# Expert stage of an adaLN mixture-of-experts layer: each 128-row half of a tile gets its own pair of experts, and the layer-one bias is read by a computed address

## The reference

```python
h = layernorm(x) * (1 + ca) + sa
x = x + ga * attn(h)               # gated linear scan, 32 x 256 tokens of 128 channels
h = layernorm(x) * (1 + cb) + sb
logits = h @ gate_w.T + gate_b      # E = 8 experts
probs = softmax(logits); topk = top_k(probs, 2)
h1 = relu(h @ w1[e] + b1[e])        # 128 -> 512, for each of the two chosen experts e
y  = h1 @ w2[e] + b2[e]             # 512 -> 128
x = x + gb * (p_a * y_a + p_b * y_b)
```

## Time and profile before

| | |
|---|---|
| median of 3 runs | 510.71 us (509.54 to 510.82) |
| the profiled execution (span from first to last instruction) | 521.0 us |
| PE busy | 418.3 us (80%) |
| DVE busy | 442.3 us (85%) |
| ACT busy | 300.5 us (58%) |
| POOL busy | 218.9 us (42%) |
| granted TensorE clock, mean | 0.896 |
| first transpose of the expert stage | 211.5 us |
| tiles run in the expert stage | 46 (92 output writes of 128 rows), 30 straight and 8 loop turns of 2 |

### The profile page before, as it was taken

How to read it: one execution, slowest core, us unless ns; L and a number is a source line. 1 busy time by engine, 2 the same in 40 slices (tenths; PEclk the granted TensorE clock), 3 DMA queues, 4 the chain that set the end, 5 groups by cost and what they waited for, 6 DMA issues and landing times.

```text
span 521.0 us, 14959 instructions
## 1 busy us (share of the span) xinstructions
PE 418.3 (80%) x4292; PEld 344.1 (66%) x4293; DVE 442.3 (85%) x1275; ACT 300.5 (58%) x757; POOL 218.9 (42%) x325
## 2 busy tenths in 40 slices
PE   2868897968865730699999999999999899999960
PEld 2435564545534630499989889998888888888860
DVE  5989999768668773999999999999999899899960
ACT  1538987677753600366667666666666555555530
POOL 7053334757776566013443333443334333333331
PEclk9969999889776555699999999999999999999985
DMA  7535443523312233313333222333223222222210
GB/s 230 160 108 163 120 151 132 184 92 124 123 63 109 111 129 141 90 46 82 88 101 104 84 76 80 80 93 86 75 76 78 76 73 67 71 73 73 67 39 0
DMA packets 48138, 51.04 MB, mean 98 GB/s; under 512 B 5454, under 2 KB 41759, under 8 KB 48082
## 3 DMA queue, kind: packets, MB, share of 16 engines
q1 hardware_dynamic: 39968, 33.17, 22.9%
q0 software_dynamic: 7040, 16.93, 9.0%
q10 hardware_dynamic: 1074, 0.23, 0.2%
HBM read 27.43 MB, written 24.70 MB: 100 GB/s over the span
## 4 chain that ended last, share of the span: by engine, by line
PE 38%; DVE 20%; issue 19%; POOL 14%; DMA 2%; another core or an unknown queue 1%; SPq 1%; ACT 1%; DVEq 0%; POOLq 0%; ACTq 0%
POOL sorted_rows L562 10%; PE bank L1468 6%; PE bank L1465 6%; PE bank L1466 6%; PE bank L1449 6%; PE bank L1451 5%; PE bank L1450 5%; DVE xs L1230 4%; PE bank L1461 2%; DVE xn L905 2%; PE bank L1435 2%; DVE hT L1243 2%; DVE st L845 2%; DVE a L1248 1%
## 5 line engine op out<-in xcount | busy, mean ns | idle before, releaser
L586 POOL DMA_INDIRECT out_dram<-tg,midx x92 | 105.9, 1151 | 199.8 <-DVE tg L1251 185.8
L748 ACT ACTIVATE xs<-bank,bcols 128x256 f32<-128x256 f32 x368 | 139.4, 492 | 22.7 <-PE bank L1451 22.3
L1465 PE MATMUL bank<-w2hi,xs 128*128 x736 | 122.7, 220 | 0.0
L1466 PE MATMUL bank<-w2hi,w2f 128*128 x736 | 122.6, 220 | 0.0
L1232 DVE TENSOR_TENSOR w2f<-xs 128x1024 f16<-128x1024 f32 x92 | 112.7, 1225 | 3.2
L1468 PE MATMUL bank<-w2lo,xs 128*128 x736 | 101.7, 220 | 0.0
L1449 PE MATMUL bank<-xh,w1hi 128*128 128x256 f16 x368 | 101.4, 276 | 0.3 <-ACT xs L748 0.3
L1450 PE MATMUL bank<-xl,w1hi 128*128 128x256 f16 x368 | 101.2, 275 | 0.0
L1451 PE MATMUL bank<-xh,w1lo 128*128 128x256 f16 x368 | 101.2, 275 | 0.0
L562 POOL DMA_INDIRECT sorted_rows<-pay,idx x64 | 64.8, 1013 | 33.4 <-issue 18.4
L758 ACT ACTIVATE xn<-bank,xs 128x128 f32<-128x128 f32 x92 | 28.7, 363 | 86.7 <-issue 48.7
(11 more groups left out here) (233 smaller groups left out, 706.1 us busy)
## 6 DMA issues: line engine op xcount, KB each, us to landing
xs<-sorted_rows SPq DMA_DIRECT2D x46, 260.0 KB
xs<-sorted_rows SPq DMA_DIRECT2D x47, 128.0 KB, 2.4
sorted_rows<-padt SPq DMA_DIRECT2D x10, 582.0 KB
w2f<-in_L_ffn_w_dram SPq DMA_DIRECT2D x4, 512.0 KB, 3.8
xs<-in_L_ffn_w_dram SPq DMA_DIRECT2D x4, 512.0 KB, 4.0
xs<-in_L_attn_x_dram SPq DMA_DIRECT2D x3, 512.0 KB, 8.6
out_dram<-tg,midx POOLq DMA_INDIRECT x92
sorted_rows<-pay,idx POOLq DMA_INDIRECT x64
```

Source lines behind the costliest of these rows:

```text
L586: pool.indirect_dma_start(out_rows, bass.IndirectOffsetOnAxis(midx[k][:, t:t + 1], 0), yout[k][:, t, :], None, bounds_check=TOK - 1, oob_i ...
L748: ins = act.activation(hf[e][:, cc, :], bank[2 * e + cc // 2][:, (cc % 2) * TW:(cc % 2 + 1) * TW], ACT.Relu, bias=bcols[n % 2][:, e * HC + ...
L1465: pe.matmul(o[t], hh[n % 2][e][:, cc, t * P:(t + 1) * P], whi, start=False, stop=False)
L1466: pe.matmul(o[t], hl[n % 2][e][:, cc, t * P:(t + 1) * P], whi, start=False, stop=False)
```

## The change

A tile stays 256 rows and two halves, but each half of 128 rows now has its own table entry: its own first row and its own pair of experts. So a pair of n tokens takes n/128 halves, rounded up, and two pairs can share a tile. Four halves (`UNITS`) make a loop turn; the number of turns comes from the number of halves, and 15 turns (30 tiles) are again written out straight. The table is computed for blocks of 128 rows in place of 256, with no more steps; the padding between pairs is 128 rows (five padding blocks in place of ten), and `row_mid`, `drop` and `kept` have one half each in place of two.

In the stage, SP's loads are one per half. Layer one runs per half: 48 matmuls over 128 columns in place of 24 over 256. Layer two has the same 52 matmuls in another order. The register instructions ahead of the weights come once per half, and `unit_experts` reads two codes per tile. On ACT the ReLU runs per half, 16 over 128 columns in place of 8 over 256, with the bias taken from `b1col` at an address computed from the expert's register, so ACT now reads the two codes too; DVE's `biases`, the tiles `bcols` and their semaphore are gone.

```diff
-SPAN = TOK + TW
+SPAN = TOK + P
@@
-MIN_TURNS = TOK // TW // BUFS
-MAX_TURNS = -(-(TOK // TW + PAIRS) // BUFS)
+UNITS = HALVES * BUFS
+MIN_TURNS = TOK // P // UNITS
+MAX_TURNS = -(-(TOK // P + PAIRS) // UNITS)
@@
-        def experts(eng, code):
-
+        def unit_experts(eng, it, n, t):
+
+            code = eng.value_load(table[1:2, bass.ds(it * UNITS + (n * HALVES + t), 1)], min_val=0, max_val=E * E - 1)
             return [code % E, code // E]
+
+        def hidden_bank(e, t, cc):
+            first = (cc % 2) * TW + t * P
+            return bank[2 * e + cc // 2][:, first:first + P]
@@
             def load_x(it, k):
-                sp.dma_start(xin[k][:, :, :], tile_rows(it, k)[:, :, 0:D]).then_inc(x_tile_in[k], 16)
+                for t in range(HALVES):
+                    sp.dma_start(xin[k][:, t, :], unit_rows(it, k, t)[:, 0:D]).then_inc(x_tile_in[k], 16)
@@
-            def hidden(it, n):
+            def hidden(it, n, ex):
                 for e in range(2):
                     act.wait_ge(hps_ready, it * (2 * BUFS) + (2 * n + e + 1))
-                    if e == 0:
-                        act.wait_ge(bcols_ready, it * BUFS + (n + 1))
                     after(act, hl_ready, it * (2 * BUFS) + (2 * n - 1 + e))
-                    for cc in range(HC):
-                        ins = act.activation(hf[e][:, cc, :], bank[2 * e + cc // 2][:, (cc % 2) * TW:(cc % 2 + 1) * TW],
-                                             ACT.Relu, bias=bcols[n % 2][:, e * HC + cc:e * HC + cc + 1])
+                    for t in range(HALVES):
+                        for cc in range(HC):
+                            ins = act.activation(hf[e][:, cc, t * P:(t + 1) * P], hidden_bank(e, t, cc),
+                                                 ACT.Relu, bias=b1col[:, bass.ds(ex[t][e] * HC + cc, 1)])
                     ins.then_inc(hf_ready, 1)
@@
-            def biases(it, n):
-                code = dve.value_load(table[1:2, bass.ds(it * BUFS + n, 1)], min_val=0, max_val=E * E - 1)
-                ins = None
-                for e, ex in enumerate(experts(dve, code)):
-                    ins = dve.tensor_copy(bcols[n % 2][:, e * HC:(e + 1) * HC], b1col[:, bass.ds(ex * HC, HC)])
-                ins.then_inc(bcols_ready, 1)
@@
             def layer1(it, n, ex):
                 pe.wait_ge(xl_ready, it * BUFS + (n + 1))
                 for e in range(2):
                     after(pe, hf_ready, it * (2 * BUFS) + (2 * n - 1 + e))
-                    for cc in range(HC):
-                        o = bank[2 * e + cc // 2][:, (cc % 2) * TW:(cc % 2 + 1) * TW]
-                        whi, wlo = (w[:, bass.ds(ex[e] * H + cc * P, P)] for w in (w1hi, w1lo))
-                        pe.matmul(o, whi, xh[n % 2][:, :], start=True, stop=False)
-                        pe.matmul(o, whi, xl[n % 2][:, :], start=False, stop=False)
-                        ins = pe.matmul(o, wlo, xh[n % 2][:, :], start=False, stop=True)
+                    for t in range(HALVES):
+                        xht, xlt = (x[n % 2][:, t * P:(t + 1) * P] for x in (xh, xl))
+                        for cc in range(HC):
+                            o = hidden_bank(e, t, cc)
+                            whi, wlo = (w[:, bass.ds(ex[t][e] * H + cc * P, P)] for w in (w1hi, w1lo))
+                            pe.matmul(o, whi, xht, start=True, stop=False)
+                            pe.matmul(o, whi, xlt, start=False, stop=False)
+                            ins = pe.matmul(o, wlo, xht, start=False, stop=True)
                     ins.then_inc(hps_ready, 1)
@@
-                    bias = b2row[:, bass.ds(ex[e] * D, D)]
                     for t in range(HALVES):
-                        pe.matmul(o[t], ones16[:, :], bias, start=True, stop=False)
-                    for cc in range(HC):
-                        whi, wlo = (w[:, bass.ds(ex[e] * H + cc * P, D)] for w in (w2hi, w2lo))
-                        for t in range(HALVES):
-                            pe.matmul(o[t], hh[n % 2][e][:, cc, t * P:(t + 1) * P], whi, start=False, stop=False)
-                            pe.matmul(o[t], hl[n % 2][e][:, cc, t * P:(t + 1) * P], whi, start=False, stop=False)
-                        for t in range(HALVES):
-                            ins = pe.matmul(o[t], hh[n % 2][e][:, cc, t * P:(t + 1) * P], wlo, start=False,
-                                            stop=(cc == HC - 1))
+                        pe.matmul(o[t], ones16[:, :], b2row[:, bass.ds(ex[t][e] * D, D)], start=True, stop=False)
+                        for cc in range(HC):
+                            whi, wlo = (w[:, bass.ds(ex[t][e] * H + cc * P, D)] for w in (w2hi, w2lo))
+                            hht, hlt = (h[n % 2][e][:, cc, t * P:(t + 1) * P] for h in (hh, hl))
+                            pe.matmul(o[t], hht, whi, start=False, stop=False)
+                            pe.matmul(o[t], hlt, whi, start=False, stop=False)
+                            ins = pe.matmul(o[t], hht, wlo, start=False, stop=(cc == HC - 1))
                 ins.then_inc(yps_ready, 1)
```

More of the change, by code:

```diff
@@ L222, in adaln_moe_kernel @@
         over = sb("over", [P, 1])
-        row_mid = sb("row_mid", [P, HALVES, P])
-        drop = sb("drop", [P, HALVES, P])
-        kept = sb("kept", [P, HALVES, P])
+        row_mid = sb("row_mid", [P, P])
+        drop = sb("drop", [P, P])
+        kept = sb("kept", [P, P])
         midx = [sb(f"midx{k}", [P, HALVES], I32) for k in range(BUFS)]
@@ L398, in _ @@
             pads = sorted_rows.rearrange("(j s) r -> s j r", s=SPAN)
-            pad_parts = [(first, j) for j in range(0, PAIRS // 2 + 1, PAD_J) for first in (0, P)]
+            pad_parts = range(0, PAIRS // 2 + 1, PAD_J)
             for g in range(NG - 4):
@@ L409, in _ @@
                 if 1 <= g <= len(pad_parts):
[L410 to L411 removed]
+                    j = pad_parts[g - 1]
+                    sp.dma_start(pads[0:P, j:j + PAD_J, :],
                                  padt[:, :].unsqueeze(1).to_broadcast([P, PAD_J, ROW])).then_inc(pad_out, 16)
@@ L439, in settled @@
             def settled(n):
-                sp.wait_ge(landed, sp.value_load(table[2:3, n:n + 1], min_val=1, max_val=2))
+                last = n * HALVES + HALVES - 1
+                sp.wait_ge(landed, sp.value_load(table[2:3, last:last + 1], min_val=1, max_val=2))
                 sp.sem_inc(sp_turn, 1)
@@ L1207, in _ @@
             dve.tensor_tensor(tcols[:, 0:1], full[:, :], sums[:, 3:4], ALU.add).then_inc(tcols_ready, 1)
-            dve.tensor_scalar(kept[:, :, :], row_mid[:, :, :], sums[:, 4:5], over[:, 0:1], ALU.mult, ALU.is_lt
+            dve.tensor_scalar(kept[:, :], row_mid[:, :], sums[:, 4:5], over[:, 0:1], ALU.mult, ALU.is_lt
                               ).then_inc(drop_made, 1)
@@ L1424, in _ @@
             pe.wait_ge(drop_made, 1)
-            for t in range(HALVES):
-                ins = pe.transpose(bank[7][:, t * P:(t + 1) * P], kept[:, t, :], ident[:, :])
-            ins.then_inc(dropT_ready, 1)
+            pe.transpose(bank[7][:, 0:P], kept[:, :], ident[:, :]).then_inc(dropT_ready, 1)
             pe.wait_ge(table_ready, 1)
@@ L1438, in experts_of @@
             def experts_of(it, n):
-                code = pe.value_load(table[1:2, bass.ds(it * BUFS + n, 1)], min_val=0, max_val=E * E - 1)
-                return experts(pe, code)
+                return [unit_experts(pe, it, n, t) for t in range(HALVES)]
             def layer1(it, n, ex):
```

66 lines of the change are left out of this document (32 added, 34 removed).

## The result

| | before | after |
|---|---|---|
| median of the timed runs, 4 each on this chip | 510.59 us (509.54 to 510.82) | 645.49 us (644.83 to 647.16) |
| ratio, 95% interval | | 1.267 (1.262 to 1.272) |
| span of the profiled execution | 521.0 us | 645.3 us |
| granted TensorE clock, mean | 0.896 | 0.857 |

The change made the kernel 134.9 us slower; the forecast was 620 us. The page of the changed kernel begins as follows (part 1: engine, busy time, share of the span, instructions), and of part 5 the output writes and the matmuls that open a half's layer two are shown.

A forecast was written before the change was run, and what follows sets the result against it. PE's instruction queue was to bound the changed kernel at 9.54 us per tile: straight part +103.1, first tile +0.3, loop +5.3, end +0.7, +109.4 on profiled 521.0 gives 630.4, carried over to 620 us; 8-in-10 range 595 to 660.

The forecast's parts named there:

- The first rival: PE's queue: register instructions cost only their printed durations, tile stays at PE's 5.75 us, kernel 476 us; chance 0.08.
- The deciding point: Expert stage: time per tile at which the changed stage (40T + 16) equals today's 285 us, T = 6.7 us.
- the price of one: PE's queue: 0.24 us per layer-one chunk, 1.1 per layer-two group, 0.65 per code load, set by register instructions.
- The choice between printed durations (78 ns) and starts (240 ns): PE's queue, layer one: price each chunk by spacing of starts, 0.24 us, not by printed 46 + 32 ns.
- the sum per tile: PE's queue per tile: layer one 3.84, layer two 4.4, two code loads 1.3, together 9.54 us.
- the loop: Loop turns of two tiles: 22.3 us each, five turns 111.5 against eight at 106.2, +5.3 us.
- the first tiles: Start of the stage: first tile, without layer two and at half clock, gains one load or so, +0.3 us.
- the other way: Second x load ahead of the first transpose: some tenths of a us, offsetting shorter table code and fewer padding blocks, net 0.
- The carry-over: Whole kernel: timed median 510.7 is 2% below profiled 521.0; that difference carried over turns 630.4 into 620 us.
- The fourth rival: PE's queue: profiler stretches register instructions 5 to 8%, tile 9.0, kernel 598 us; counted within the forecast's 0.72.
- second rival: PE's clock falls to 1.2 GHz on thin work: 11.1 us a tile, kernel 684 us; chance 0.10.
- third rival: ACT is last: sixteen ReLUs at the upper 8.5 us (lower 4.2), 10.8 us a tile, 670 us; chance 0.07.

The follow-up runs named there:

- the first experiment: The changed kernel with both halves using the first half's pair of experts, one code read per tile on PE, same matmuls: 479.98 us, ratio 0.945 to the kernel before.

## Why the prediction was right, and where it was off

**Right: what decides.** PE's queue is the bound, by its register instructions. Halving them on the same matmuls gave 480 us; adding only them to the kernel before gave 625. The first rival (the queue keeps out of the way) forecast 476 us, and that is what the kernel would have been: 480 with the queue's work halved, but the pace of the queue did not fall. The deciding point, 6.7 us per tile, lies between that run's 6.1 and the changed kernel's 10.14.

**Right: the price of one.** 0.24 us per chunk of layer one, 1.1 per group of layer two, 0.65 for a load: the differences between the runs give 1.94 for eight chunks (10.14 - 8.20) and 0.61 for a load. The choice between printed durations (78 ns) and starts (240 ns) carried the forecast. The Trainium skill, page "Perfetto Trace Analysis", section "Sequencer-only Instruction", has the profile show only the execution of such an instruction; the spacing of L1450's sixteen starts agrees, 0.26 us with 46 + 32 ns printed.

**Off: the sum per tile,** 9.54 for 10.14. This is the step that failed in size, and 0.6 x 29 = 17 us of the 25 missed. By the starts in PE's queue, over the 24 tiles from 242 to 485 us, the forecast's terms measure as follows: layer one 4.22 (forecast 3.84), from the first load to layer two's first register instruction 1.43 (1.3), from there to the next tile's layer one 4.48 (4.4). Most of the miss is layer one's price per chunk, 0.264 and not 0.24; the two bare waits per tile, 0.11 each, had no term. The regular step from one register instruction to the next has its forecast length, but about once in each us of queue time one comes 20 to 155 ns late, as at 306.52: 0.5 us per tile. The FUSED_REGOPS at the first chunk of a half, up to 96 ns printed for 46, add 0.2. Both stand in the trace of before as well, where the array hid them, and the forecast's prices held a part of them; but I had read layer one's pace from eight instructions whose starts are rounded to 0.1 us. The forecast should have taken it from a longer stretch. What causes the late starts no run here settles.

**Off: the loop,** 22.3 for 23.5. It is the same term: 2 x 10.14 and 3.2 us for the head, against 2 x 9.54 and 3.2. The head (branch, two more loads, address rows) was right as a sum; its parts were not measured one by one.

**Off: the first tiles,** +0.3 for +3.7. I had looked only at "one load or so". The third tile's transpose waited 2.58 us for its x rows, which the trace of before does not show at that place. This is not the queue price of PE: with PE's register instructions halved (the first experiment) the first three tiles take 10.9 us and the wait is 2.70. It is SP. Its transfers up to the third tile's x rows, in the changed kernel and then before (timeline of SP):

```profile
197.17 4.44 SPq L430 DMA_DIRECT2D xs<-sorted_rows  x4
202.40 4.57 SPq L434 DMA_DIRECT2D xs<-sorted_rows  x4
208.45 4.30 SPq L430 DMA_DIRECT2D xs<-sorted_rows  x4
...
209.34 2.22 SPq L424 DMA_DIRECT2D xs<-sorted_rows  x2
212.33 1.56 SPq L427 DMA_DIRECT2D xs<-sorted_rows  x2
215.81 2.23 SPq L424 DMA_DIRECT2D xs<-sorted_rows  x2
```

Eight transfers go ahead of the third tile's now, and four did before. They leave SP's queue 1.1 us apart or more, so the third tile's first one leaves 7.8 us after the first transpose, where it was 4.3. The forecast had put the second x load "the other way" at some tenths and set the whole term to nothing; the straight part hides SP's loads, the first tiles don't.

**The carry-over.** The forecast set its sum on the profiled execution and then took off the ten us by which that one was longer. It gave no reason why they would be absent from the changed kernel, so that this came out right was luck. The fourth rival (the profiler stretches the queue) would have made the tile shorter outside the profile, but the changed kernel's profile (645.3) and its timed runs (645.5) agree. The ten us of before's profile lay ahead of the expert stage.

**The clock** (second rival). It dipped as that rival's text allowed, 0.93 in the straight part, and cost nothing. Eleven tiles at full clock, and six with stretches at half clock (same columns as above):

```profile
312.83:424.30 111.47, 96.57 (x1125) 75.47 (x1124) 62.73 (x110) 58.25 (x209) 21.92 (x22) 1.00 0.21 53
434.64:495.56 60.92, 52.65 (x615) 46.42 (x613) 34.22 (x60) 31.76 (x114) 14.10 (x12) 0.83 0.21 52
```

They take 10.13 and 10.15 us a tile. At half clock matmuls of 128 columns start 0.11 apart (those from 302.77 to 303.31), and the queue leaves each about 0.1, so what PE loses in such a stretch it makes up while it waits for the loads.

**ACT** (third rival). Sixteen ReLUs took 4.23 us; the lower bound was 4.2, the upper 8.5. A register instruction ahead of an ACT instruction is hidden by the one before.

## What to carry to other kernels

Ask of an engine not only how long its instructions take but what its queue does per instruction: a register instruction that computes an address cost PE's queue about 0.12 us here, whether one, two or four matmuls follow it, a load of a register 0.65, and both are free only as long as the matmuls behind them last longer. A finer unit of work with its own addresses doubles them, so compare queue time per unit with engine time per unit before halving the unit. Values that a loop turn has already computed are cheaper kept in registers than read again at the head. A version that takes the two halves' addresses once where their experts are the same, and apart only in the mixed tiles, might keep a part of the gain of 40 tiles; it wasn't tried.

## What the runs showed of the hardware that was not expected

- The queue's late starts described above: 205 in the 243 us from 242.5 to 485.5, 0.5 us of each tile, with register instructions and loads of otherwise fixed length. They differ in size, but their places are not random: from one to the next there are 32 of PE's instructions (register instructions, weight loads and matmuls, in the program's order) in 110 of 204 cases and 30 to 32 in 147. Their cause no run here shows. They cost nothing while the engine is the bound.
- Moving a load in a queue that has little slack moves the gap with it (0.40 and 1.07 us where the loads went, for 1.08 and 0.3); two loads less at the head, one of them put back in mid-turn, shortened the turn by 1.4.
- The branch at the end of a turn, in PE's queue (the run with the registers kept):

```profile
L1482 PEldq COMPARE_BRANCH  x8: 83/227/284, 383.1 to 466.5; - x8
...
L1482 PEldq BRANCH_PREFETCH_HINT  x1: 36/36/36, 383.5 to 383.5; - x1
```

The first line is the whole loop, the second the first turn's end. The first branch is 284 ns long, and 0.34 us pass from its start to the next instruction; the median is 227, and the 83 is the last, which leaves the loop. The Trainium skill, page "Advanced Engine Details and Errata", section "Control Flow Timing", gives about 108 ns for a compare-and-branch; here a branch back is two to nearly three times that, and the measurement decides.
